# A hybrid of three layers on one core: the state-space part unrolled, its decay matrices made as exponentials of differences of running sums

## What is computed

```
xBC = silu(causal_conv4(x @ W_xBC))        # 512 channels: x (256), B (128), C (128)
dt  = softplus(x @ W_dt + dt_bias)         # one number per token and head
dA  = dt * (-exp(A_log));  dA_cs = cumsum(dA) within chunks of 32 tokens
y_i = sum over j <= i of (C_i . B_j) * decay(j -> i) * dt_j * x_j   +  D * x_i
decay(j -> i) = exp(sum of the steps of the cumulated dA from j to i)
out = rmsnorm(y * silu(z)) @ W_out
```

## Time and profile before

| what | value |
|---|---|
| time, median of 3 runs | 1023.21 us (1020.62 to 1023.95) |
| profiled execution: its own time | 1023.41 us |
| profiled execution: span from first to last instruction | 1021.5 us |
| busy over the span: PE, PEld, DVE, ACT, POOL | 86%, 66%, 73%, 47%, 41% |
| granted PE clock, mean over the span | 0.948 |

### The profile page before, as it was taken

The page is one execution under the profiler, slowest core; times in us unless marked ns, Lnnn a source line. Parts: engine busy times, 40 slices in busy tenths (PEclk is TensorE's granted clock), DMA queues, the critical chain, the costliest instruction groups (busy, mean ns, idle before and its releaser), DMA issues.

```text
span 1021.5 us, 18311 instructions
## 1 busy us (share of the span) xinstructions
PE 878.5 (86%) x5538; PEld 678.3 (66%) x5538; DVE 747.0 (73%) x1982; ACT 475.8 (47%) x943; POOL 416.2 (41%) x748
## 2 busy tenths in 40 slices
PE   2589999999998979996978698887868797978998
PEld 1478888888887747774646466565646464655776
DVE  1457667667765357776799888989898988947785
ACT  2234344443443357774544344444435353426775
POOL 0456656656565111210444343443435344442221
PEclk9879999999998999997899988999999898988999
DMA  8222121121221000000000000000000000000112
GB/s 225 76 49 58 45 62 36 47 60 37 49 58 36 24 1 0 0 0 2 1 1 2 0 0 0 0 0 0 0 0 0 0 0 0 0 1 21 41 41 63
DMA packets 75027, 26.37 MB, mean 26 GB/s; under 512 B 29536, under 2 KB 74720, under 8 KB 74976
## 3 DMA queue, kind: packets, MB, share of 16 engines
q1 hardware_dynamic: 74976, 25.72, 9.8%
HBM read 15.23 MB, written 10.49 MB: 25 GB/s over the span
## 4 chain that ended last, share of the span: by engine, by line
PE 53%; issue 19%; DVE 9%; POOL 7%; ACT 3%; DMA 3%; POOLq 0%; ACTq 0%; DVEq 0%; SPq 0%
PE bank L1382 8%; PE bank L1362 4%; PE bank L1361 4%; PE bank L1427 3%; POOL arena L525 3%; PE bank L1542 2%; PE bank L1473 2%; PE bank L1195 2%; PE bank L1188 2%; PE bank L1276 2%; PE bank L1290 2%; PE bank L1257 2%; DVE arena L1029 2%; PE bank L1170 2%; PE bank L1527 1%
## 5 line engine op out<-in xcount | busy, mean ns | idle before, releaser
L525 POOL TENSOR_TENSOR arena<-arena 128x768 f32<-128x768 f32 x64 | 115.6, 1809 | 155.3 <-ACT arena L745 77.8
L1039 DVE TENSOR_TENSOR_SCAN arena<-bank,tab 128x256 f32<-128x256 f32 (+1 forms) x256 | 121.1, 534 | 32.4 <-PE bank L1461 31.5
L1029 DVE SCALAR_TENSOR_TENSOR arena<-bank,convw_sb,arena 128x510 f32<-128x510 f32 (+2 forms) x192 | 135.4, 732 | 2.0 <-ACT arena L692 2.0
L448 POOL TENSOR_TENSOR var_eps<-mv,eps_cols 128x4 f32<-128x4 f32 x66 | 13.3, 201 | 258.9 <-DVE mv L769 188.7
L1473 PE MATMUL bank<-arena 128*64 128x256 f32 x256 | 86.7, 423 | 28.7 <-POOL arena L525 28.6
L1382 PEld LDWEIGHTS bank<-downT,ff 128*128 128x128 f32 x768 | 89.5, 192 | 8.1 <-DVE ff L956 5.8
L1382 PE MATMUL bank<-downT,ff 128*128 128x128 f32 x768 | 91.3, 275 | 1.7 <-DVE ff L956 1.5
L579 ACT ACTIVATE ff<-bank 128x256 f32<-128x256 f32 (+2 forms) x112 | 46.1, 412 | 83.1 <-PE bank L1195 34.4
L663 ACT ACTIVATE ff<-bank 128x512 f32<-128x512 f32 x96 | 56.8, 592 | 58.9 <-PE bank L1362 57.8
L698 ACT ACTIVATE arena<-arena 128x512 f32<-128x512 f32 x64 | 39.7, 622 | 91.2 <-DVE arena L1029 91.2
L562 ACT ACTIVATE xn<-x_all,shift,rstd 128x128 f32 (+1 forms) x192 | 78.5, 481 | 0.0
(11 more groups left out here) (166 smaller groups left out, 2041.4 us busy)
## 6 DMA issues: line engine op xcount, KB each, us to landing
LT_dram<-arena SPq DMA_DIRECT2D x16, 256.0 KB, 2.3
ff<-T_dram SPq DMA_DIRECT2D x16, 256.0 KB, 3.0
ff<-R_dram SPq DMA_DIRECT2D x16, 256.0 KB, 3.3
out<-x_all SPq DMA_DIRECT2D x8, 512.0 KB, 3.2
x_all<-in_L_attn_a_x SPq DMA_DIRECT2D x7, 512.0 KB, 7.0
x_all<-in_L_attn_a_x SPq DMA_DIRECT2D x2, 256.0 KB, 3.2
T_dram<-tab SPq DMA_DIRECT2D x2, 256.0 KB, 2.7
R_dram<-tab SPq DMA_DIRECT2D x2, 256.0 KB, 3.4
```

The lines of the kernel that those rows point to most:

```text
L525: nc.gpsimd.tensor_tensor(score[h % 2][u], cb[u], hgam[h % 2][u], ALU.mult).then_inc(score_done[u], 1)
L1029: nc.vector.scalar_tensor_tensor(acc, src, convw_sb[:, q, TAPS - 1 - s:TAPS - s], acc, ALU.mult, ALU.add).then_inc(tap_done[v], 1)
L1039: last = nc.vector.tensor_tensor_scan(hgam[h % 2][u][:, strip(b, c)], bank[u][(3, 0)[h % 2]][:, b * SEQ + c * P:(b + 1) * SEQ], eye_zero[: ...
```

## The change

The loop is gone: `space_half(b, e, f, x, d)` is written out 18 times, and half `h` begins group `b = h`, makes scores and head outputs of group `e = h-1`, and finishes group `f = h-2` (sums of squares, projection, addition). The layernorm runs seven groups ahead (`x = h+7`, `xnT` has 8 buffers instead of 4) and the dt projection six ahead (`d = h+6`). The PSUM banks are shared by task instead of by stream: two for the convolutions, two for gates, transposes, products and dt (`mid_bank`), two for the log decays (`step_bank`), two for y (`y_bank`).

dt chain: the softplus runs over 64 columns, once for four groups (a quad), spread over four halves: `softplus_begin` (1 operation), `softplus_middle` (5) and `softplus_end` (10) with `chunk_sums` (2 scans), `running_sums` (7 operations on 32 rows by 256), `split_sums` (6 of the same size). The steps of a sequence are cumulated as exact sums of coarse and fine parts and written as three fp16 pieces; SP stores these to DRAM and loads them into the rows of two fp16 tiles (nine transfers for a quad), whose other rows hold constant weights, set once by POOL (`set_rows`).

Decay: for each head and sequence PE adds, in one bank of `step_bank`, a constant fp16 matmul (384 columns, -30000 above the diagonal, exp of which is 0) and two matmuls over 6 rows (256 and 128 columns) that give the difference of the running sums (`log_decay`); ACT takes the exponential of the 384 columns (`decay_of`). The scans of DVE, the spreading transposes of PE and the transpose back are gone. `head_outputs(r)` makes the outputs of heads 2r and 2r+1 with the matmuls of the two alternating. Squares of the two halves of y are added on POOL (one operation of 512 columns more), so the sums of squares need 4 matmuls instead of 8.

Order of one full half on each engine:

- PE: conv 0, conv 1, log_decay 0, gate 0, log_decay 1, sums of squares of f, gate 1, log_decay 2, projection of f, log_decay 3, conv 2 (waits for the last tap of block 0), conv 3 (the same of block 1), head_outputs 0, token_major 0 and 1, transposes of x, dt projection of d, head_outputs 1, products 0 and 1 (wait for SiLU of block 3).
- ACT: first_tap 0 and 1, decay_of 0 to 3 (8 exponentials), first_tap 2, silu_z 0 and 1, first_tap 3, silu_x 0 and 1, normalise x, square 0, copy of xnT, silu_x 2 and 3, two copies of C.B, square 1.
- POOL: the two operations of layernorm of x, the power for f (waits for the sums of squares), four scores, two gate products, the sum of squares.
- DVE: as in the diff below.

Ahead of half 0 stands a new prologue with nothing of a group in it: layernorm of groups 2 to 6, dt of groups 0 to 5, the whole dt chain of quad 0, and `set_rows`. On DVE its order is: stats 2, bias 0, stats 3, bias 1, shift 2, stats 4, shift 3, bias 2, stats 5, shift 4, bias 3, softplus_begin, stats 6, shift 5, softplus_middle, softplus_end, shift 6, bias 4, bias 5, chunk_sums, running_sums, split_sums. PE has transposes(g) and then the dt projection of g-1, for g from 2 to 6, and waits for chunk_sums before half 0; ACT has normalise(g) and then the copy of xnT(g-1); POOL has the layernorm of 2 to 4, `set_rows(0)`, the layernorm of 5 and 6, `set_rows(1)`. DVE also makes four small fp16 constants.

The core of the diff (the lines of before are those printed above):

```diff
+            for q in range(GROUPS // QUAD):
+                side = q % 2
+                sp.wait_ge(chain_step, CHAIN * (q + 1))
+                if q >= 2:
+                    sp.wait_ge(pieces_in, 16 * 2 * QUAD * (q - 1))
+                sp.dma_start(pieces_dram[side].rearrange("m r c -> r m c"), pieces[:, :, :]).then_inc(pieces_out, 16)
+                sp.wait_ge(pieces_out, 16 * (q + 1))
+                sp.wait_ge(rows_set, 4)
+                sp.wait_ge(E_mm, past(2 * HEADS * QUAD * (q - 1) - 1))
+                for j in range(QUAD):
+                    src = pieces_dram[side][:, j * BATCHES * HEADS:(j + 1) * BATCHES * HEADS, :].rearrange("m r c -> m (r c)")
+                    sp.dma_start(from_rows[side][32 * j:32 * j + 2 * PIECES:2, :], src).then_inc(pieces_in, 16)
+                    sp.dma_start(to_rows[side][32 * j + 1:32 * j + 1 + 2 * PIECES:2, :], src).then_inc(pieces_in, 16)
...
+            def set_rows(side):
+                for dst, weight in ((from_rows[side], from_side), (to_rows[side], to_side)):
+                    nc.gpsimd.tensor_copy(dst, weight.broadcast_to([P, 4 * GROUP])).then_inc(rows_set, 1)
...
+                def decay_of(h):
+                    for batch in range(BATCHES):
+                        act.wait_ge(E_mm, done(2 * HEADS * e + 2 * h + batch))
+                        act.wait_ge(score_done, past(HEADS * (e - 1) + h))
+                        nc.scalar.activation(hgam[h][:, batch * TRI:(batch + 1) * TRI], step_bank[batch][:, 0:TRI],
+                                             ACT.Exp).then_inc(hgam_done, 1)
...
-                def head_decay(h):
-                    dve.wait_ge(habc_mm[u], nth(HEADS * iu + h + 1))
-                    dve.wait_ge(score_done[u], nth(HEADS * iu + (h - 1 if h >= 2 else 0)))
-                    for b in range(BATCHES):
-                        for c in range(2):
-                            last = nc.vector.tensor_tensor_scan(
-                                hgam[h % 2][u][:, strip(b, c)], bank[u][(3, 0)[h % 2]][:, b * SEQ + c * P:(b + 1) * SEQ],
-                                eye_zero[:, 0:SEQ - c * P], 0.0, ALU.mult, ALU.add)
-                    last.then_inc(hgam_done[u], 1)
...
+                begin_q, end_q, sums_q, split_q = quads
+                if x is not None:
+                    stats_at(*x)
+                if split_q is not None:
+                    split_sums(split_q)
+                if b is not None:
+                    taps(1, 0, 1)
+                if f is not None:
+                    dve.wait_ge(ms_mm, done(f))
+                    dve.wait_ge(rms_done, past(f - 2))
+                    nc.vector.tensor_scalar(ms[f % 2], y_bank[1][:, 0:GROUP_TILES], 1.0 / INNER, RMS_EPS,
+                                            ALU.mult, ALU.add).then_inc(ms_done, 1)
+                if b is not None:
                     taps(2, 0, 1)
+                if x is not None:
+                    shift_at(*x)
+                if f is not None:
+                    add_residual(f)
+                if b is not None:
+                    taps(3, 0, 1)
+                if sums_q is not None:
+                    running_sums(sums_q)
+                if end_q is not None:
+                    softplus_middle(end_q)
+                if b is not None:
+                    taps(1, 2, 3)
+                if e is not None:
                     skip(0)
+                if b is not None:
                     times_dt(0)
                     times_dt(1)
+                if end_q is not None:
+                    softplus_end(end_q)
+                if b is not None:
+                    taps(2, 2, 3)
+                    taps(3, 2, 3)
+                if d is not None:
+                    with_bias(d)
+                if begin_q is not None:
+                    softplus_begin(begin_q)
+                if e is not None:
+                    skip(1)
+                if end_q is not None:
+                    chunk_sums(end_q)
...
+                def log_decay(h):
+                    j, side = e % QUAD, e // QUAD % 2
+                    rows = slice(32 * j, 32 * j + 2 * PIECES)
+                    for batch in range(BATCHES):
+                        to = step_bank[batch]
+                        a = (batch * HEADS + h) * SEQ
+                        pe.wait_ge(hgam_done, past(2 * HEADS * e + 2 * h + batch - 2))
+                        mm(to[:, 0:TRI], ident16[:, :], never16[:, :], start=True, stop=False)
+                        mm(to[:, 0:SEQ], from_rows[side][rows, a:a + P], to_rows[side][rows, a:a + SEQ],
+                           start=False, stop=False)
+                        mm(to[:, SEQ:TRI], from_rows[side][rows, a + P:a + SEQ], to_rows[side][rows, a + P:a + SEQ],
+                           start=False, stop=True).then_inc(E_mm, 1)
+                def head_outputs(r):
+                    pe.wait_ge(score_done, done(HEADS * e + 2 * r + 1))
+                    if r == 0:
+                        pe.wait_ge(x_done, past(2 * GROUPS + e - 1))
+                        pe.wait_ge(xt_done, done(INNER_BLOCKS * e + 1))
+                    else:
+                        pe.wait_ge(ms_done, past(e - 1))
+                    x_of = tile4(xt[e % 2])
+                    for batch in range(BATCHES):
+                        for c in range(2):
+                            for k in range(2):
+                                h = 2 * r + k
+                                last = mm(y_bank[r][k * HEAD_DIM:(k + 1) * HEAD_DIM, batch * SEQ + c * P:(batch + 1) * SEQ],
+                                          x_of[:, 2 * batch + c, h * HEAD_DIM:(h + 1) * HEAD_DIM], score[h][:, strip(batch, c)],
+                                          start=(c == 0), stop=(c == 1))
+                    last.then_inc(hy_mm, 1)
...
-                def spread_decay(w, it, h):
...
-                    for t in range(GROUP_TILES):
-                        at = t * HEADS + h
-                        last = nc.tensor.transpose(bank[w][(3, 0)[h % 2]][:, cols(t)],
-                                                   of_stream[:, at:at + 1].broadcast_to([P, P]), ident)
-                    last.then_inc(habc_mm[w], 1)
```

More of the change, by code:

```diff
@@ L542, in _ @@
+            for g in range(2, LN_LEAD):
+                ln_rstd_of(2 * GROUPS + g, g)
+                if g == QUAD:
+                    pool.wait_ge(x_done, done(2 * GROUPS - 1))
+                    set_rows(0)
+            set_rows(1)
+            for h in range(SSD_HALVES):
+                space_half(*ssd_half(h))
             ffn(1)
@@ L1141, in space_half @@
+                if e is not None:
+                    skip(0)
+                if b is not None:
                     times_dt(0)
                     times_dt(1)
[L1143 to L1148 removed]
@@ L1159, in _ @@
+            running_sums(0)
+            split_sums(0)
+            for h in range(SSD_HALVES):
+                space_half(*ssd_half(h), [quad_at(h, stage) for stage in range(QUAD)])
             ffn(1)
@@ new lines, in space_half @@
+                if b is not None:
+                    gate(1)
+                if e is not None:
+                    log_decay(2)
+                if f is not None:
+                    pe.wait_ge(yT_done, done(INNER_BLOCKS * f + 1))
+                    for t in range(GROUP_TILES):
+                        for r in range(INNER_BLOCKS):
+                            last = mm(y_bank[0][:, cols(t)], yT[r][f % 2][:, cols(t)], wout_sb[:, r, :],
+                                      start=(r == 0), stop=(r == INNER_BLOCKS - 1))
+                    last.then_inc(out_mm, 1)
```

702 lines of the change are left out of this document (368 added, 334 removed).

## The result

The change made the kernel slower: 1067.6 and 1068.0 us in two runs against a median of 1021.9, ratio **1.0443** [1.0409, 1.0477]. Two further runs took 1085 and 1087 us at a mean granted clock of 0.88 where these two had 0.90; they are left out of the ratio, no trace of them was kept, and why they were longer is not shown. I had forecast 1034 with a range of 1008 to 1057. The sign was right, the size was not: +46 us in place of +11.

A forecast was written before the change was run, and what follows sets the result against it. It took a ring PE, DVE, POOL, PE with DVE nearly full to bound the old kernel, and the order through ACT the new. Loop -18 and start +29 gave +11 on 1023.4, so 1034 us, range 1008 to 1057.

The forecast's parts named there:

- walk of one full half: One half, followed engine by engine from PE's first conv: 25.5 us, with PE working some 20.5 of them.
- the rival that ends faster: In the halves, full clock and log_decay at 0.7 us a head: 23.9 us a half, about 1010 in all; chance 0.28.
- the ring: Chain of waits between engines setting a half's 25.5 us: ring after ring through ACT with its two table loads.
- The start: Layer start to the end of half 0: 52 us instead of 23.3, so +29 (25 to 34).
- The end: Last two halves, mostly the serial run from scores to addition: 25 us.
- log_decay: PE's decay matmuls: 0.55 us a sequence, 1.1 a head, with bounds of 0.7 and 1.4 a head.
- Head pairs: PE's head outputs: two heads on different array halves overlap, 1.4 us a pair instead of 2.7.
- The dt chain: Quads 1 to 3: softplus_end 2.2, chunk_sums 0.8 and one wait add 3.3 us for each of three halves, 10 us.
- The drain of a table load: Rival on ACT: each load also drains about 1.38 us, 2.8 us a half, some 42 in all, 1076; chance 0.02.
- Head pairs do not overlap: Rival on PE's head outputs: 2.7 us a pair, 26.6 us a half, 1051 in all; chance 0.16.
- DVE waiting beside POOL: Rival in the dt chains: ten two-SBUF operations wait 1.4 us each while POOL works, 1054 in all; chance 0.08.

The follow-up runs named there:

- fill_both: Changed kernel with 18 extra identity matmuls a half in PE's waits of 0.91, 2.14, 0.96 and 0.65 us, no wait removed: 1041.9 us, ratio 1.0198.
- prologue: Changed kernel with DVE's list ahead of half 0 reordered, statistics and shifts ahead of the dt bias additions: 1080.1 us, ratio 1.0559.
- early: Changed kernel with two one-column activations a half (Silu behind the decays, Exp behind the last Silu), loading each table ahead of use: 1019.5 us, ratio 0.9957.
- early_chain: early with the chain's exponential first on ACT, and softplus_middle, softplus_end and running_sums moved behind first taps and residual addition: 1012.4 us, ratio 0.9901.
- best: early_chain with the DVE order of prologue, and the third taps put ahead of the shift and residual addition: 1009.5 us, ratio 0.9889.
- best2: best with softplus_end put back behind times_dt, its place in the changed kernel: 1014.6 us, ratio 0.9906.
- early_fill: early with 10 extra identity matmuls a half (3, 3 and 4, in PE's waits of 0.91, 0.72 and 0.97 us): 1013.2 us, ratio 0.9907.
- best2_fill: best2 with 10 extra identity matmuls a half, 6 ahead of the first token-major transpose and 4 ahead of the transposes of x: 1002.9 us, ratio 0.9817.
- fill: Changed kernel with 15 extra identity matmuls a half in PE's waits of 0.91, 2.14 and 0.96 us: 1072.9 us, ratio 1.0456.
- early_nopair: early with head outputs written head after head, four matmuls each, instead of two heads alternating: 1017.5 us, ratio 0.9962.

## Why the prediction was wrong

*The step that failed* is the walk of one full half, in its price for PE. The walk took each of PE's durations at full clock or near it, and I named the clock only in the rival that ends faster ("idle spells in it are at most 2.3 us against the granted 0.94 of before"). The walk itself had found the waits of 0.8 us ahead of log_decay 1 and 2.3 us ahead of the transposes, and had moved the ring onto PE. It did not ask what such waits do to an engine whose clock is granted. They cost it half its speed for 7 to 8 us each (714.24 to 722 and 732 to 739.3 in the half shown).

The check is `fill_both`. Its halves 2 to 15 run from 544.79 to 911.07 us, 366.3 us, with a granted clock of 1.00 in eight of them; the walk's figure was 357 and 10 for the chains, 367. In the changed kernel they take 391.9. These 25.6 us are the clock's, with the filling's own work in the shorter time. By the sum of the misses (36) they are 70% of it; half 1, 4.0 over, is of the same kind (25.0 us at a clock of 0.80, where `prologue` has 21.5 at 0.99 with the same instructions in it). That 366 is so near to 367 is luck: plain halves at full clock are 24.85, not 25.5, and the rest is made up by a half of `fill_both` that fell to 0.87 and five at 0.94 to 0.98.

*The other terms.* The start: 56.4 for 52, with the ring of one group after another and DVE's order in it as walked; `prologue` shows that 5.7 us of its prologue, 4.7 up to half 1, were the order alone. The end: 28.2 for 25, at a clock of 0.70. log_decay: 0.53 a sequence for 0.55. Head pairs: 1.52 for 1.4, they do overlap. The dt chain: in `fill_both` its two halves take 27.31 and 25.53 against two plain ones of 24.85, 3.1 us for the 3.3 told, by luck too: the three terms named for it, 2.2, 0.8 and a wait of 1.25, add up to 4.2, and the third chain, at 0.87 and 0.94, takes 30.19 and 27.14 against plain halves of some 26. In faster halves it costs more, 26.43 and 25.60 against 22.60 in `early`, partly by the clock.

*The rivals.* The faster one had the right mechanism with the wrong sign: a clock that stays full is worth 26 us here, but the kernel's own waits see to it that it doesn't. Its time of 1010 is near what `early_chain` reaches once both loads are off the ring. The drain of a table load (1076) would have been close to the measured time and is still wrong. In the timeline of ACT in the changed kernel the activation ahead of the load ends at 711.31, and the next one begins 1.30 us after the load's start:

```profile
711.33 1.28 ACT L783 ACT_TABLE_LOAD   x1
712.63 0.87 ACT L783 ACTIVATE arena<-bank 128x384 f32<-128x384 f32 x2
```

The drain that the Trainium skill tells of ("ScalarE: Activation LUTs", What ACT_TABLE_LOAD costs) isn't there; a load costs the 1.30 us, and through PE's clock more: both together 48 us over 16 halves, 3.0 a half, of which 1.95 are latency by the waits. "Head pairs do not overlap" was wrong in the mechanism, and its price was wrong too: without overlap a pair takes 2.22 us, not 2.7, and the half grows by 0.2, not 1.1. DVE waiting beside POOL is not needed to explain the changed kernel's loss; it showed itself in `best` (4.52 us for six small operations), and taking it away in `best2` gained nothing.

*Left open.* Why the last halves keep a clock of 0.92 to 0.93 in `early_fill` and `best2_fill`, and when a wait brings the clock down: the same 0.66 us did not do it in all halves of the changed kernel (plain halves of 27.2 us have one fall, that of 30.7 has two), plain halves of `early` stay at 1.00 with waits of 0.91, 0.72 and 0.97 us, and `prologue` shows that the history counts. In the chain's half of `best2_fill` (0.94 and 26.2 us) the wait can be named: PE stands idle 2.31 us for DVE ahead of the chain's transposes, at 654.00, and the products behind it take 2.91 us where they took 1.57.

## What to carry to other kernels

When a change empties the engine that was full and makes the ring turn on TensorE, walk the new order at both levels of its clock, and list its waits: each is a possible fall, and the price is what stands behind it, not its own length. Look at the clock column of each stretch before explaining a long one; if two stretches with the same PE instructions differ by their PE busy time and by that column, it is the clock. Two cheap tests are worth their place early: load an activation table ahead of use with a one-column activation (48 us here), and fill a wait with matmuls into columns that nobody reads (26 us here, 7 to 12 in `best2`). Fill all the waits of a loop, for some of them alone may give nothing (`fill`).

## What was not expected of the hardware

- A row of like halves has more than one period with the same PE instructions: 22.8 and 24.5 us in `early_nopair`, 27.2 and 30.7 us in the changed kernel and in `prologue`, each at its own granted clock (1.00 and 0.93; 0.87 and 0.72 to 0.78). With a prologue 5.7 us shorter the long one came in more halves, and the whole took 12 us more.
- More work can be less time: 18 extra matmuls a half, 24.19 us busy in place of 22.51, and a half of 24.85 in place of 27.18 us.
- Eight one-column matmuls in a row (1.05 us) do not lower the clock if no wait stands ahead of them.
